# Moving two input copies of a recurrence, one of its loads, and two groups of matmuls in a fused SSM, MLP and FP4 kernel

## The reference, cut to what matters

```
xn = layernorm(x)
out = x + attn(xn) + ffn(xn)

attn(v):  v = v + ssm_scan(rmsnorm(v, scale1))        # 512 channels x 16 states, a recurrence over time
          h = rmsnorm(v, scale2)
          return v + gelu(h @ w1 + b1) @ w2 + b2      # 512 -> 2048 -> 512
ffn(v):   gate = fp4(v) @ fp4(w_gate).T ; y = fp4(v) @ fp4(w_up).T      # 512 -> 1408
          return fp4(silu(gate) * y) @ fp4(w_down).T                     # 1408 -> 512
fp4(v):   blocks of 16 along the last axis: scale = max|v|/6, nearest of 0, .5, 1, 1.5, 2, 3, 4, 6
```

## Time and profile before

| | |
|---|---|
| median of 3 runs | 3157.8 us (3156.46 to 3161.61) |
| profiled execution, its own time | 3159.74 us |
| its span, first to last instruction | 3157.9 us |
| mean granted TensorE clock | 0.998 |
| PE busy | 3067.0 us, 97% |
| DVE busy | 2046.9 us, 65% |
| ACT busy | 1088.4 us, 34% |
| POOL busy | 1146.3 us, 36% |

### The profile page before, as it was taken

How to read it: one execution, slowest core, us unless ns; L and a number is a source line. 1 busy time by engine, 2 the same in 40 slices (tenths; PEclk the granted TensorE clock), 3 DMA queues, 4 the chain that set the end, 5 groups by cost and what they waited for, 6 DMA issues and landing times.

```text
span 3157.9 us, 43122 instructions
## 1 busy us (share of the span) xinstructions
PE 3067.0 (97%) x14861; PEld 2472.7 (78%) x14861; DVE 2046.9 (65%) x4427; ACT 1088.4 (34%) x1910; POOL 1146.3 (36%) x1097
## 2 busy tenths in 40 slices
PE   5899999999999999999999999999999999999999
PEld 3678888888877777777777788888888888888887
DVE  8798898987777766767777754444445444454442
ACT  5445655645444333333422321212122121121211
POOL 7556656655555544545554210110011111111000
PEclk9999999999999999999999999999999999999999
DMA  4133434357766656666643533333333333333320
GB/s 123 45 92 86 119 112 122 92 138 184 186 176 166 162 152 170 158 157 171 163 99 94 127 72 71 73 73 71 78 67 79 74 68 71 71 73 74 71 60 14
DMA packets 865577, 335.58 MB, mean 106 GB/s; under 512 B 680400, under 2 KB 771792, under 8 KB 862800
## 3 DMA queue, kind: packets, MB, share of 16 engines
q1 hardware_dynamic: 865360, 332.83, 43.1%
HBM read 225.21 MB, written 107.51 MB: 105 GB/s over the span
## 4 chain that ended last, share of the span: by engine, by line
PE 69%; DVE 15%; issue 5%; POOL 4%; DMA 3%; SPq 2%; ACT 2%; DVEq 0%; POOLq 0%; ACTq 0%
PE bank L875 22%; PE bank L891 22%; PE bank L752 14%; PE bank L774 7%; DVE qs L995 3%; POOL qa L1541 2%; DVE qa L1012 2%; PE bank L815 2%; DVE qs L1006 1%; DVE qa L968 1%; DVE qb L1020 1%; POOL qa L1535 1%; PE bank L823 1%; SPq L493 1%; PE bank L722 1%
## 5 line engine op out<-in xcount | busy, mean ns | idle before, releaser
L875 PE MATMUL bank<-hT,Wp 128*128 128x512 f32 x3072 | 744.9, 391 | 2.4 <-DVE Wp L1182 2.4
L891 PE MATMUL bank<-Wp,G 128*128 128x512 f32 x3072 | 744.0, 391 | 0.0
L875 PEld LDWEIGHTS bank<-hT,Wp 128*128 128x128 f32 x3072 | 577.3, 188 | 128.1 <-issue 2.8
L891 PEld LDWEIGHTS bank<-Wp,G 128*128 128x128 f32 x3072 | 576.9, 188 | 126.3
L752 PE MATMUL bank<-XT,Wg 128*128 128x512 f32 (+1 forms) x2148 | 526.8, 394 | 10.6 <-DVE Wd L1027 5.4
L752 PE MATMUL bank<-XT,Wu 128*128 128x512 f32 (+1 forms) x2148 | 514.1, 388 | 15.9 <-DVE sg L960 15.6
L774 PE MATMUL bank<-Wd,HT 128*128 128x512 f32 x2112 | 515.6, 393 | 6.8 <-POOL HT L1549 6.3
L1231 DVE CAST G<-gf 128x512 fp32r<-128x512 f32 x256 | 110.8, 433 | 608.9 <-PE bank L891 589.8
L752 PEld LDWEIGHTS bank<-XT,Wu 128*128 128x128 f32 x2148 | 400.1, 189 | 106.3 <-issue 25.7
L752 PEld LDWEIGHTS bank<-XT,Wg 128*128 128x128 f32 x2148 | 400.1, 191 | 100.7 <-issue 12.3
L774 PEld LDWEIGHTS bank<-Wd,HT 128*128 128x128 f32 x2112 | 391.7, 188 | 106.0 <-issue 14.3
(11 more groups left out here) (114 smaller groups left out, 2829.5 us busy)
## 6 DMA issues: line engine op xcount, KB each, us to landing
px<-in_L_attn_x_dram SPq DMA_DIRECT2D x128, 256.0 KB, 3.3
xin<-in_L_attn_x_dram SPq DMA_DIRECT2D x128, 256.0 KB, 3.6
sT<-r_K SPq DMA_DIRECT2D x128, 256.0 KB, 4.1
r_Z<-xin SPq DMA_DIRECT2D x64, 256.0 KB, 2.4
r_U<-ub SPq DMA_DIRECT2D x16, 1024.0 KB, 6.7
sU<-r_U SPq DMA_DIRECT2D x32, 512.0 KB, 5.3
r_Y<-sY SPq DMA_DIRECT2D x16, 1024.0 KB, 5.6
xl<-in_L_attn_x_dram SPq DMA_DIRECT2D x64, 256.0 KB, 3.1
```

Source lines behind the costliest of these rows:

```text
L875: ins = e.matmul(bk[:], Wp[f][wh][:, 0, k * P:(k + 1) * P], hT[xh][b % 2][:, k, :], start=(k == 0 and p_ == 0), stop=(k == KD - 1 and p_ = ...
L891: ins = e.matmul(ACC[j][:], G2[gh][:, n % 2, j * P:(j + 1) * P], Wp[f][wh][:, 1, :], start=(f == 0 and p_ == 0), stop=(f == 15 and p_ == 2))
```

## The change

Three moves; nothing is added or removed.

- SP: `u_load(2)` goes from window 99 (`k == 0`, behind `tile_back`) to window 100 (`k == 1`), in front of `v_load(1)` and `tw_load(1)`. Loads 3 to 31 stay.
- ACT: `ssm_inputs(0)` goes from window 98 to window 99, `ssm_inputs(1)` from window 99 to window 100, in front of `ssm_result(0)`. Copies 2 to 31 stay.
- PE: `mlp1(0)` goes from window 179 to window 178, in front of `down(176)`; `mlp1(1)` goes from behind `down(177)` to in front of it.

```
@@ sync_program, window(s)
                 if 0 <= k < 2 * NV:
                     v = k // 2
-                    if k % 2 == 0 and v + 2 < NV:
+                    if k == 1 or k >= 2 and k % 2 == 0 and v + 2 < NV:
                         u_load(v + 2)
@@ tensor_program, window(s)
-                if s >= NW:
-                    mlp1(s - NW)
+                if NW - 1 <= s <= NW:
+                    mlp1(s - NW + 1)
                 if 2 <= s <= NW:
                     down(s - 2)
@@ scalar_program, window(s)
-                if k == -1:
-                    ssm_inputs(0)
-                if 0 <= k < 2 * NV - 2 and k % 2 == 0:
+                if 0 <= k < 2:
+                    ssm_inputs(k)
+                elif k < 2 * NV - 2 and k > 0 and k % 2 == 0:
                     ssm_inputs(k // 2 + 1)
                 if 0 <= k < 2 * NV and k % 2:
                     ssm_result(k // 2)
```

## The result

The changed kernel takes 3162.96 us in the median of 20 runs (3160.99 to 3166.25), the kernel before 3158.97 us in 20 runs of the same study (3156.46 to 3161.61). The ratio is 1.0013 with a 95% interval of 1.0007 to 1.0019: 4.0 us slower (2.2 to 6.0). The forecast was +5.9 us, 3163.7 us for the median, in a range of 3158.5 to 3167.5 us that holds both.

A forecast was written before the change was run, and what follows sets the result against it. The prediction took PE, busy 97% of the span, to bound the kernel. A 6.9 us delay in the recurrence less 1.0 us gained at the seam gave 3157.8 + 5.9 = 3163.7 us, range 3158.5 to 3167.5 us.

The forecast's parts named there:

- Steps 2 and 3: Window 99: PE's states wait 1.3 us for ACT's copy 0; SP stands 5.2 us longer for it before u_load(1).
- Step 4: End of window 99: tile 96's read-back, queued behind u_load(1), lands late, making DVE 4.5 us late (3.6 to 5.0).
- Step 5: Window 100: PE's second half of the outputs waits for DVE's scan, 4.5 us late, the 1.3 us included.
- Step 6: Window 100: u_load(2) waits for copy 1, so tw_load(1) begins 6.9 us late, adding 2.4 us (2.2 to 2.9).
- Step 7: Window 101's x load, behind tw_load(1), has no cover: DVE and PE's up product are 6.9 us late.
- Step 8: After that all five streams stay 6.9 us late; PE's waits up to 1740 give nothing back.
- The rival by which it is swallowed: PE's later waits for DVE absorb the 6.9 us before 1740, leaving the 1.0 us gain: 3156.8 us; chance 0.10.
- the one with the first delay only: tw_load(1) catches up or window 101's x load lands sooner: +3.5 us in all, 3161.3 us; chance 0.10.
- the third load: The delay repeats at the x tile of window 103, 2.4 us more: +8.3 us, 3166.1 us; chance 0.05.
- The seam: Seam of the two halves, window 178 on: PE's 1.01 us wait before down(177) goes, gaining 1.0 us (0.7 to 1.0).
- The clock rival: PE's new stalls at 961 and 981: a clock fall at the second costs up to 1.5 us, 3165.2; chance 0.15.
- The sum: Whole kernel: +6.9 - 1.0 = +5.9 us, bounds +4.8 to +7.2, 3163.7 us for the median.

The follow-up runs named there:

- e3: Changed kernel with u_load(1) at the end of SP's window 98, behind tile_back(96) and tile_out(97): 3159.67 us against 3160.06 before, ratio 1.0001.
- e2: Kernel before with only the moves of copies 0 and 1 and of load 2, PE's seam untouched: 3164.28 us against 3160.06, ratio 1.0014.
- e8: The changed kernel measured and profiled again, nothing altered: 3164.96 us against 3160.22 for the kernel before, ratio 1.0016.
- e7: Changed kernel with SP's x load of window 101 ahead of u_load(2), v_load(1), tw_load(1): 3161.56 us against 3160.22 for the kernel before, ratio 1.0005.
- e6: Kernel before with PE's mlp1 moves and all the recurrence's x loads ahead of its other loads on SP: 3148.12 us against 3160.22, ratio 0.9962.
- e4: As e3, and SP's x load of window 101 ahead of u_load(2), v_load(1), tw_load(1): 3157.73 us against 3160.06 for the kernel before, ratio 0.9992.
- e1: Kernel before with only PE's moves of mlp1(0) and mlp1(1): 3158.39 us against 3160.06, ratio 0.9998.
- e5: Kernel before with PE's mlp1 moves and SP's x load of window 101 ahead of v_load(1) and tw_load(1): 3158.16 us against 3160.22, ratio 0.9993.

## Why the prediction was right, step by step

- **Steps 2 and 3 held.** PE's wait in front of the states was 1.08 us (predicted 1.3), and `u_load(1)` started 8.16 us after `h_mult(98)` instead of 3.10: 5.06 us late (predicted 5.2).
- **Step 4 held, its size was off.** I took 3.2 us to the landing of the last read-back; it was 2.7 to 2.9 in all four profiles with this delay. So DVE was late by 3.97 us and PE's outputs by 3.9, not by 4.5. It was nearer to the low end of the earlier trace rows than I chose. That this is because SP had stood, so that nothing but `u_load(1)` was in front of it, is my reading; no run changes it alone.
- **Step 5 held** (no slack at the scan: PE's delay is DVE's to 0.1 us), and e3 shows the cause.
- **Step 6 held, a little smaller.** `tw_load(1)` was late by 5.9 us, 2.0 more than the first delay (predicted 2.4), mostly since `u_load(2)` took 0.33 us to issue, not 0.62. In e2 and e8 it was late by 7.1 and 6.4, but the x load behind it by 6.3 and 6.7 (6.0 in the first profile).
- **Step 7 held.** By window 104 the delay was 6.6, 5.75 and 7.7 us in three profiles (predicted 6.9); the differences between them lie in how long the x load took to land, 4.5, 3.4 and 4.9 us (3.9 before). The step has this landing at 3.9, without a range of its own; it is what made the second delay 2.7, 1.8 and 3.9 us.
- **Step 8 held.** From window 104 to 170 the three took 676.20, 675.65 and 675.58 us, against 675.07: nothing is given back. At the seam PE begins `mlp1(0)` 803.0 us after `h_mult(98)`, where it began `down(176)` after 795.0 before: 8.0 us late (6.9 predicted, wrong outside 4 to 10), of which 1.4 arose between windows 104 and 177. The rival by which it is swallowed, and the one with the first delay only, fall. So does the third load: DVE does not stand for the x tile of window 103 in any of them.
- **The seam** brought 1.1 to 1.2 us (predicted 1.0), by the steps given, `gelu(1)` in front of `h_high(178)` included.
- **The clock rival** was half right. The clock fell at the first of the two new stalls in all four profiles that have it (changed, e2, e7, e8). From the outputs' second half to the gate product of window 101 PE then took 7.7 us in the first profile and 6.5 in the others, against 4.9 before. Where the second stall follows, this costs nothing in the end, as the prediction has it: PE was 6.66 us late in window 101 already, so the second stall had gone (0.3 us was left of it in e2). In e7, which has no second stall, it costs 1.6 us. Only in e8 did the clock fall at the second stall too.
- **The sum.** 6.6 - 1.2 = +5.4 from the first profile, 5.75 - 1.1 = +4.6 from e2; measured 4.0 (2.2 to 6.0) and 5.1 (2.2 to 7.9). What is between 5.4 and 4.0 is inside the measurement's uncertainty, and the profiles name no place for it. The bounds of the terms, +4.8 to +7.2, leave the first measurement's 4.0 out. That the forecast's 3163.7 us is only 0.7 above the measured 3162.96 is partly luck: the loss was taken 1.9 too large, and the base, the median of three runs (3157.8), was 1.2 below that of the twenty (3158.97). I had also taken 6.3 us for the least that a measurement can tell from no change; with twenty runs the interval of the 4.0 us is clear of zero.

What the prediction said of the kernel before was incomplete in one thing that e6 shows: DVE's five waits for x loads were worth far more than the whole change. The rows for one of them were there; I used it as missing cover and didn't ask what it cost in itself.

## What to carry to other kernels

An instruction that is moved for one engine's sake takes its semaphore with it: look for a DMA on an in-order issuing stream that waits for it, and then for what stands behind that DMA. Put loads and read-backs whose data is wanted soon and whose buffers are free ahead of those that have to wait; here that order, more than the copies, made the loss of 4 to 5 us, and it made about 9 of e6's 12 us of gain. A wait of a feeding engine is worth to the bounding engine only what that one stands itself, so read both timelines before pricing it.

## What the runs showed of the hardware

- With a stall of PE of 2.7 to 2.8 us at window 100 the granted clock went to half (1.2 GHz instead of 2.4) in four of four profiles. After the stall behind the seam it fell with 2.41 and 3.09 us (before, e4) and 2.29 us (e8), and not with 2.29, 2.36 and 2.41 us (e7, e1, e5) nor with 1.53 to 1.93 us (e3, changed, e6, e2). Between 1160 and 1215 us it fell with 1.93 (e4), 2.19 (e5), 2.33 and 2.41 (e1), 2.45 (e2) and 2.50 us (e7), and not with 2.30 (changed) and 2.42 us (e8), nor with 1.40 to 1.95 us in eight other waits. So the length of a stall alone does not tell here; a fall behind the seam costs 1.5 us (12 matmuls in 4.45 us instead of 2.93), and it comes or not from one execution to the next, which is part of the scatter of this kernel's times. The Trainium skill (TensorE: Matmul & The Clock Gate, Part 1: The HAM clock gate) names idleness as what brings half clock; the traces agree, since each of the fourteen falls between 940 and 1790 us in the ten profiles came with a wait of PE of 1.93 to 3.09 us.
- The same four DMAs of 64 KB each (`tile_back(96)`) landed 3.3 to 3.8 us after the last issue when they followed the recurrence's twelve loads and `u_load(1)` on the queue, 2.7 to 2.9 us when SP had stood before `u_load(1)`, and 2.5 to 2.9 us when they were issued right behind the twelve loads, in front of `u_load(1)` (e3, e4).
